# A selective scan's preparation, moved one slot ahead in a hand-written order of three interleaved streams

## The chip, the core and the metric

One core of a Trainium2 chip runs the whole program. Its engines work side by side, each on its own queue in order: TensorE (PE; its weight loads, PEld, overlap with it), VectorE (DVE), ScalarE (ACT), GpSimd (POOL) and SyncE (SP), which issues the DMAs. Semaphores tie them together. The metric is the time of the program on the device in microseconds (us).

## The reference

The input is 8 sequences of 512 tokens, 128 wide. Six layers run one after the other: a mixture of 8 experts (ffn 0), a Mamba layer, ffn 0 again, a second mixture of experts, windowed attention, and that mixture again. The change touches the Mamba layer, which for each sequence computes, cut to what matters:

```
h  = layernorm(layernorm(x)) * gamma + beta      # 512 tokens x 128
xi, z = split(h @ in_proj_w)                     # 256 wide each
xi = silu(causal_conv4(xi) + conv_b)             # four taps for each channel
dt, B, C = split(xi @ x_proj_w)                  # 8, 16, 16 wide
dt = softplus(dt @ dt_proj_w + dt_proj_b)
state = exp(dt * A) * state + (dt * xi) * B      # 16 states for each channel, token by token
y  = (sum over states of state * C) + xi * D
out = gelu((y * silu(z)) @ out_proj_w); gated linear unit; + skip
```

The first ffn 0 must be done with a sequence before Mamba prepares it, and the second ffn 0 follows Mamba on it.

## The kernel before

The first half of the program is the function `front`. It weaves three streams: A (ffn 0, first time), M (Mamba, function `mamba`) and F (ffn 0, second time). Time is cut into slots. On each engine's queue the instructions stand slot by slot, and within a slot in the order A, M, F. There is no barrier between slots; a slot is a place in the order, and each engine runs as far ahead as its semaphores let it.

**A and F.** One step is one 128-wide piece of one expert's hidden layer: three matmuls of 128x512 up (L123 to L125, PE), a relu (L390, ACT), and, two steps later, the product down, four 128x128 blocks in eight matmuls (L359, PE). After every fourth step DVE adds the expert's result, weighted, to the residual (L418). A sequence is 32 steps. F makes one step a slot, from slot 110 on. A's steps per slot are given by `pace`: 1 up to slot 56 but for two slots with 2, then 5 in 3 slots up to 110, then 4 in 5. A's last step comes near slot 244. Late in F and A one bank of PSUM each holds the up product and one the down product, so the next up product waits for the relu, and the next expert's down product for DVE's accumulation.

**M.** Sequence s takes the slots 56 + 32 s to 87 + 32 s; "slot 12 of sequence 3" is the 13th of these. The streams of M are written with v = slot - 56. In each slot, one of 16 states and one half (128 channels) of the inner width are worked on: ACT makes the decay exp(dt * A) one slot ahead (L798), POOL makes db = du * B three ahead (L808), DVE scans (L813) and multiplies by C (L828, `times_c`), and two slots later POOL adds the product to y (L839). SP loads B and C rows spread over the partitions (L529).

Beside this, M prepares the next sequence, s + 1, during sequence s, and ends the last one, s - 1. The class `Side` does it: a preparation is a generator per engine, and a tuple of slot numbers says in which slots its pieces are issued. `PREP_PE`, `PREP_ACT`, `PREP_DVE` and `PREP_POOL` are those of the preparation, the `TAIL_` tuples those of the end. The pieces of the preparation, in the order of the data:

- DVE: statistics and mean (L74, L80). It waits for A to be done with the sequence. POOL: six small operations to scales (L591 to L598).
- ACT: xm, the normalised tokens (L659, four activations). PE: T, four transposes (L114). DVE: hT (L716).
- PE: in0 (L626). DVE: c03 to c00, the four taps of half 0 (L723, L726), which read PSUM and u. ACT: t0, a tanh (L666). The same for half 1: in1, c13 to c10, t1. Between t0 and t1 ACT makes skip (L672).
- DVE: u0 and u1, the second step of silu (L730).
- PE: x, the product with x_proj_w (L634, two fp32 products in four matmul records). It waits for u1. ACT: two copies out of PSUM (L680 is one). DVE: lo, the small part of dt for a second product (L733). SP: B and C rows go to DRAM at slot 23.
- PE: dt0, dt1. ACT: the steps to softplus. DVE: sp0, sp1 (L737) in slot 28. POOL: du (L602). PE: in2, in3, the z part (L649), ACT and DVE after it.

All products of the preparation and the tail use one bank, XM. The tail of s - 1 has the output product (L748) in PE's slot 5, the two gated products gl0 and gl1 (L758, L759) in slots 6 and 8, ACT's gelu and two tanhs (sg0, sg1, L776) in slots 5, 6 and 8, DVE's go0 and go1 (L789) in slots 7 and 9. T must wait for go1, the last to read the bank. In M's part of a slot the tail's piece stands ahead of the preparation's.

F's own preparation for its next sequence falls, by its offsets, into M's slots 12 to 19: on DVE its statistics in 12, four small operations in 17 and four in 19; its accumulation is in every slot 3, 7, 11, 15, 19 and so on.

Of the kernel before, what the change touches and what calls it, by code (L numbers as in the profile page):

```python
# [222 lines left out]
def ffn0(S, C, sb, W, tag, x_at, x_ready, acc_at, acc_ready, hbank, ybank, HB, YB, XB, late=0):  # L223
# [23 lines left out]

    PREP_PE, PREP_ACT, PREP_POOL = (25, 27), (24, 25, 25, 28), (23,)
    PREP_DVE = (22, 22, 25, 27, 27, 27, 27, 29, 29, 29, 29)
    SLOTS = range(-12, END + 7)  # L250
# [82 lines left out]
    def pe(eng):  # L333
        side = Side(eng, prep_pe, PREP_PE)
        for v in SLOTS:
# [43 lines left out]
    def act(eng):  # L379
        side = Side(eng, prep_act, PREP_ACT)  # L380
        for v in SLOTS:
            s, j = divmod(v, NJ)
            if 0 <= v < END:
                e, c = divmod(j, HC)
                if v == 0:
                    eng.wait_ge(W["b1_at"].sem, W["b1_at"].at(0))
                if v >= NR:
                    eng.wait_ge(y_done.sem, y_done.at(v - NR))
                eng.wait_ge(up_done.sem, up_done.at(v))
                eng.activation(hf[v % NR][:], HB[hbank(v)].psum[:], ACT.Relu, bias=W["b1"][:, e, c:c + 1]).then_inc(relu.sem)  # L390
                if j == 2:
                    if s >= 1:
                        eng.wait_ge(bias_p.sem, bias_p.at(s - 1, "mm"))
                    eng.wait_ge(bias_p.sem, bias_p.at(s, "T"))
                    eng.copy(mkT[:], XB.psum[0:NT * E, 0:P]).then_inc(bias_a.sem)
            side.step(v)
            yield

    def dve(eng):
        side = Side(eng, prep_dve, PREP_DVE)  # L400
        for v in SLOTS:
            J = v - LEAD - late
            s, j = divmod(J, NJ)
            if 0 <= J < END:
                e, c = divmod(j, HC)
                q = s % 2
                if c == HC - 1:
                    eng.wait_ge(y_done.sem, y_done.at(J))
                    if e == 0:
                        eng.wait_ge(pd.sem, pd.at(s, "mk"))  # L410
                        eng.wait_ge(*acc_ready(s))
                    elif e == 1:
                        eng.wait_ge(bias_d.sem, bias_d.at(s))
                    else:
                        eng.wait_ge(acc_done.sem, acc_done.at(s * E + e - 1))
                    Y = YB[ybank(J // HC)].psum
                    for k in range(NT):
                        x = eng.scalar_tensor_tensor(acc_at(s)[:, k, :], Y[:, k * P:(k + 1) * P], mk[q][:, k, e:e + 1], acc_at(s)[:, k, :], ALU.mult, ALU.add)  # L418
                    x.then_inc(acc_done.sem)
                if j == HC:  # L420
                    eng.wait_ge(bias_p.sem, bias_p.at(s, "mm"))
                    eng.wait_ge(acc_done.sem, acc_done.at(s * E))
                    eng.tensor_tensor(acc_at(s)[:], acc_at(s)[:], XB.psum[:].rearrange("p (k d) -> p k d", d=D), ALU.add).then_inc(bias_d.sem)
            side.step(v)
            yield

    def pool(eng):
        side = Side(eng, prep_pool, PREP_POOL)
        for v in SLOTS:
            side.step(v)  # L430
            yield
# [11 lines left out]
def mamba(S, C, sb, a, cleared, x_at, x_ready, o_at, o_free, rows_dram, DH, XM):  # L443
# [51 lines left out]

    PREP_PE = (10, 12, 16, 21, 23, 25, 27, 30)
    PREP_ACT = (9, 15, 17, 19, 22, 22, 24, 24, 24, 25, 26, 26, 27, 27, 27, 30)
    PREP_DVE = (7, 7, 11, 13, 13, 14, 14, 17, 17, 18, 18, 19, 20, 22, 28, 28, 29, 31)  # L500
    PREP_POOL = (8, 28, 28)
    TAIL_PE, TAIL_ACT, TAIL_DVE, TAIL_POOL = (5, 6, 8), (5, 6, 8), (1, 1, 7, 9), (2, 2, 10)
    SLOTS = range(-NJ, END + 11)

# [46 lines left out]
    def pool(eng):  # L551
# [25 lines left out]
        eng.wait_ge(zeroed.sem, zeroed.at(0, "b_lo"))  # L577
        side, late = Side(eng, prep_pool, PREP_POOL), Side(eng, tail_pool, TAIL_POOL, 1)
        for v in SLOTS:
# [261 lines left out]
    def pe(eng):  # L841
        side, late = Side(eng, prep_pe, PREP_PE), Side(eng, tail_pe, TAIL_PE, 1)
        for v in SLOTS:
            if v == -NJ:
                eng.wait_ge(vec_ld.sem, vec_ld.at(4))
                eng.transpose(XM.psum[:, 0:8], rows[0:8, :], C["ident"][0:8, 0:8]).then_inc(rows_T.sem)
                XM.free = (ready.sem, ready.at(0, "cols"))
            late.step(v)
            side.step(v)
            yield  # L850

    def act(eng):
        side, late = Side(eng, prep_act, PREP_ACT), Side(eng, tail_act, TAIL_ACT, 1)
        for v in SLOTS:
            if v == -NJ:
                eng.wait_ge(mat_ld.sem, mat_ld.at(13))
                eng.activation(a_neg[:], a_neg[:], ACT.Exp).then_inc(a_exp.sem)
            if 0 <= v + 1 < END:
                decay(eng, v + 1)
            late.step(v)  # L860
            side.step(v)
            yield

    def dve(eng):
        side, late = Side(eng, prep_dve, PREP_DVE), Side(eng, tail_dve, TAIL_DVE, 1)
        for v in SLOTS:
            if v == -NJ:
                eng.wait_ge(rows_T.sem, rows_T.at(0))
                eng.tensor_copy(cols[:], XM.psum[:, 0:8]).then_inc(ready.sem)
                eng.wait_ge(ready.sem, ready.at(0, "cols"))  # L870
                eng.tensor_scalar(cols[:, DV:DV + NH], cols[:, DV:DV + NH], 0.5, None, ALU.mult).then_inc(ready.sem)
                eng.wait_ge(a_exp.sem, a_exp.at(0))
                eng.tensor_scalar(a_neg[:], a_neg[:], -1.0, None, ALU.mult).then_inc(ready.sem)
            if 0 <= v < END:
                scan(eng, v)
            if 0 <= v < END:
                times_c(eng, v)
            late.step(v)
            side.step(v)
            yield  # L880
# [13 lines left out]
def front(nc, S, C, bank, lasting, xin, a, f0, K, w1, sorted_rows):  # L894
# [3 lines left out]
    NJ, LM, LB = E * HC, 56, 110  # L898
# [3 lines left out]
    def pace(slot):  # L902
        if slot < LM:

            return 1 + (LM - 27 <= slot < LM - 25)
        return 1 + (slot % 3 != 0) if slot < LB else int(slot % 5 != 0)

    with ExitStack() as ctx, ExitStack() as scan_ctx:
# [16 lines left out]


        slots_of_first = [slot for slot in range(-12, 2 * END) for _ in range(pace(slot))]

        def slot_of_first(v):
# [9 lines left out]

        padding = S.count("f0_padding_cleared", 1, ("w_x", "w_dt", "b2"))  # L940
        M = mamba(S, C, sb_scan, a, padding, x_of, lambda s: A["done"](s), x_of, lambda s: M["x_read"](s), rows_dram, DH, XM)
        scan_end = nc.sbuf_base
        scan_ctx.close()
# [48 lines left out]
        def pool(eng):  # L992
            eng.memset(zero_row[:], 0.0).then_inc(zeroed.sem)
            weave((-12, A["pool"](eng), pace), (0, split_experts(eng)), (LM - NJ, M["pool"](eng)), (LB - 12, F["pool"](eng)))
            eng.wait_ge(*M["done"](NSEQ - 1))
            for i, e in enumerate([E] + list(range(E))):
                for u in range(NU):
                    k, hi, lo = NU * i + u, K["up_hi"][u][:, e, :], K["up_lo"][u][:, e, :]
                    eng.wait_ge(raw_ld[k % 4].sem, raw_ld[k % 4].at(k // 4))
                    eng.tensor_copy(hi, A["spent"][k % 4]).then_inc(split.sem)  # L1000
                    eng.wait_ge(split.sem, split.at(k, "hi"))
                    eng.tensor_tensor(lo, A["spent"][k % 4], hi.bitcast(F32), ALU.subtract).then_inc(split.sem)
# [20 lines left out]
        def act(eng):  # L1023
            weave((-12, A["act"](eng), pace), (LM - NJ, M["act"](eng)), (LB - 12, F["act"](eng)), (LN, norms_act(eng)))
# [1229 lines left out]
```

## Time and profile before

The median of three runs is 1887.43 us (1886.67 to 1887.5).

| what | value |
|---|---|
| time of the profiled execution | 1886.88 us |
| its span, first to last instruction | 1885.1 us |
| PE busy, share of the span | 1736.4 us, 92% |
| DVE busy | 1255.5 us, 67% |
| ACT busy | 1101.3 us, 58% |
| POOL busy | 1208.4 us, 64% |
| first and last scan (L813) start | 129.9 and 1019.8 us |
| POOL adds a product into y (L839), 240 times | mean 1.306 us |
| mean granted clock of PE | 0.976 of full speed |

The profile is one execution. A busy share is an average over stages with different limits. "Idle before" is the time an engine stood before an instruction, with what ended it; idle time of an engine that isn't the bound of its stage costs nothing. The granted clock is 1.0 at 2.4 GHz and 0.5 at 1.2 GHz; a stretch that has some of both lies between. The scans take 890 of the 1885 us; the front ends at 1117, and the second mixture and attention follow, which the change doesn't touch.

### The profile page before, as it was taken

The numbers are of one execution on the slowest core, as the hardware profiler recorded it, in microseconds if no ns is written. First come the engines' busy times: TensorE is split into PE (matmuls) and PEld (weight loads), VectorE is DVE, ScalarE is ACT, GpSimd is POOL, SyncE is SP. The second block draws the span as 40 slices with busy tenths as digits, with TensorE's granted clock in tenths as the row PEclk, the third lists the DMA queues.
The fourth block names the chain that finished last, engine by engine and source line by source line (L and its number), as shares of the span: only waits on it lengthen the run. The fifth ranks groups of instructions, "written<-read, shape, count | busy, mean of one in ns | idle before, by whom it ended". The sixth has DMA issues, their size and how long they took to land. (4 is left out here: it accounts for less than half of the span.)

```text
span 1885.1 us, 35637 instructions
## 1 busy us (share of the span) xinstructions
PE 1736.4 (92%) x12089; PEld 1507.4 (80%) x12089; DVE 1255.5 (67%) x2932; ACT 1101.3 (58%) x1937; POOL 1208.4 (64%) x1199
## 2 busy tenths in 40 slices
PE   7999898898989989988788999999899999999998
PEld 6888777787877777876567887888799999987887
DVE  2358889777797877879887437444477766656443
ACT  3476766666656766666665554343577777653442
POOL 3238787776777867779897716465556555544663
PEclk9999999999999999999889999999899999999999
DMA  5023333332223233332231501112454435201113
GB/s 148 1 75 116 101 105 94 98 97 90 97 83 112 94 104 93 93 99 85 84 95 42 151 7 50 36 48 62 137 179 140 123 114 155 68 21 39 47 50 103
DMA packets 121358, 166.71 MB, mean 88 GB/s; under 512 B 14646, under 2 KB 56604, under 8 KB 121180
## 3 DMA queue, kind: packets, MB, share of 16 engines
q1 hardware_dynamic: 114140, 148.82, 25.9%
q0 software_dynamic: 7040, 15.60, 2.6%
q8 instruction: 101, 1.65, 0.4%
q14 instruction: 77, 0.63, 0.1%
HBM read 114.17 MB, written 50.20 MB: 87 GB/s over the span
## 5 line engine op out<-in xcount | busy, mean ns | idle before, releaser
L808 POOL TENSOR_TENSOR db<-du_m,bt 128x512 f32<-128x512 f32 x256 | 328.4, 1284 | 140.9 <-DVE bank L813 140.4
L813 DVE TENSOR_TENSOR_SCAN bank<-bank,db 128x512 f32<-128x512 f32 x256 | 312.5, 1221 | 11.4 <-ACT bank L798 11.2
L839 POOL TENSOR_TENSOR y_m<-y_m,ph 128x512 f32<-128x512 f32 x240 | 313.4, 1306 | 0.3 <-DVE ph L828 0.3
L798 ACT ACTIVATE bank<-dt_m,a_neg 128x512 f32<-128x512 f32 x256 | 176.1, 688 | 84.9 <-DVE ph L828 78.9
L828 DVE TENSOR_TENSOR ph<-bank,ct 128x512 f32<-128x512 f32 x240 | 165.9, 691 | 8.6 <-POOL y_m L839 0.5
L1329 POOL TENSOR_TENSOR s_a<-s_a,mx_a 128x768 f32<-128x768 f32 x64 | 94.2, 1472 | 87.1 <-DVE mx_a L1412 87.1
L1443 PE MATMUL bank<-vb_a,pT_a 96*128 96x64 f32 x1024 | 121.6, 272 | 0.0
L1443 PEld LDWEIGHTS bank<-vb_a,pT_a 96*128 96x128 f32 x1024 | 119.6, 192 | 0.1
L359 PEld LDWEIGHTS bank<-dn,hf1b 128*128 128x128 f32 x680 | 91.2, 196 | 17.5 <-DVE x_all L418 7.8
L359 PEld LDWEIGHTS bank<-dn,hf2b 128*128 128x128 f32 x680 | 91.3, 196 | 16.4 <-DVE x_all L418 6.6
L359 PE MATMUL bank<-dn,hf1b 128*128 128x128 f32 x680 | 92.8, 281 | 7.9 <-DVE x_all L418 6.0
L359 PEld LDWEIGHTS bank<-dn,hf0b 128*128 128x128 f32 x688 | 90.6, 193 | 11.2 <-DVE x_all L418 2.7
L359 PE MATMUL bank<-dn,hf2b 128*128 128x128 f32 x680 | 92.7, 280 | 7.0 <-DVE x_all L418 4.9
L359 PEld LDWEIGHTS bank<-dn,hf1a 128*128 128x128 f32 x680 | 91.7, 196 | 8.1 <-DVE x_all L418 0.4
L359 PEld LDWEIGHTS bank<-dn,hf2a 128*128 128x128 f32 x680 | 90.7, 194 | 7.6
L359 PEld LDWEIGHTS bank<-dn,hf0a 128*128 128x128 f32 x688 | 90.0, 191 | 7.5 <-DVE x_all L418 0.2
L359 PE MATMUL bank<-dn,hf0b 128*128 128x128 f32 x688 | 92.0, 277 | 2.0 <-DVE x_all L418 1.5
L359 PE MATMUL bank<-dn,hf1a 128*128 128x128 f32 x680 | 92.1, 280 | 0.0
L359 PE MATMUL bank<-dn,hf2a 128*128 128x128 f32 x680 | 91.1, 278 | 0.0
L390 ACT ACTIVATE hf0a<-bank,b 128x512 f32<-128x512 f32 x86 | 58.9, 685 | 55.0 <-PE bank L125 54.5
L359 PE MATMUL bank<-dn,hf0a 128*128 128x128 f32 x688 | 90.6, 275 | 0.0
L390 ACT ACTIVATE hf1a<-bank,b 128x512 f32<-128x512 f32 x85 | 58.2, 685 | 53.2 <-PE bank L125 53.1
(469 smaller groups left out, 4872.9 us busy)
## 6 DMA issues: line engine op xcount, KB each, us to landing
bt<-bc_rows SPq DMA_DIRECT2D x128, 256.0 KB, 3.5
ct<-bc_rows SPq DMA_DIRECT2D x128, 256.0 KB, 3.4
sorted<-zero_row SPq DMA_DIRECT2D x64, 288.0 KB, 4.0
k_strips_a<-k_rows SPq DMA_DIRECT2D x32, 256.0 KB, 3.1
q_strips_a<-q_rows SPq DMA_DIRECT2D x32, 256.0 KB, 3.8
q_rows<-q_hi_a SPq DMA_DIRECT2D x16, 256.0 KB, 3.0
q_rows<-q_lo_a SPq DMA_DIRECT2D x16, 256.0 KB, 3.2
k_rows<-k_hi_a SPq DMA_DIRECT2D x16, 256.0 KB, 3.3
```

What stands on the lines that cost most here:

```text
L359: x = eng.matmul(Y.psum[:, t], hf[r][:, t], W["dn"][:, e, c, :], start=c == 0 and k == 0, stop=c == HC - 1 and k == NT - 1, skip_group_che ...
L390: eng.activation(hf[v % NR][:], HB[hbank(v)].psum[:], ACT.Relu, bias=W["b1"][:, e, c:c + 1]).then_inc(relu.sem)
L798: eng.activation(DH[J % 2][:], dt[s % 2][:, j % NH, :], ACT.Exp, scale=a_neg[:, j % NH, j // NH:j // NH + 1]).then_inc(da_done.sem)
L808: eng.tensor_tensor(db[J % RD][:], du[s % 2][:, j % NH, :], bt[N % RB][:], ALU.mult).then_inc(db_done.sem)
L813: eng.tensor_tensor_scan(DH[J % 2][:], DH[J % 2][:], db[J % RD][:], 0.0, ALU.mult, ALU.add).then_inc(hs_done.sem)
L828: eng.tensor_tensor(out, DH[J % 2][:], ct[N % RB][:], ALU.mult).then_inc(ph_done.sem)
L839: eng.tensor_tensor(y[s % 2][:, j % NH, :], y[s % 2][:, j % NH, :], ph[J % RP][:], ALU.add).then_inc(ys_done.sem)
L1329: eng.tensor_tensor(X[:], X[:], M[:, :, None].to_broadcast([P, UB, KW]), ALU.subtract).then_inc(sub_done.sem)
L1443: x = eng.matmul(BO[:, at:at + 2 * GD], pT[u % 2][:, c * BB + j, :], vb[s % 2][:, b:NB + 1:NB - b, g * GD:(g + 1) * GD], start=True, stop= ...
```

## The change

Every piece of the preparation from the statistics up to u1 is issued one slot earlier, on all four engines: T, in0, in1 on PE; xm, t0, skip, t1 on ACT; everything from the statistics to u1 on DVE; the scales on POOL. x on PE and what comes after it stay in their slots. So that A is still done with sequence 0 before M's first statistics, which now come one slot earlier (slot 30), A makes two steps in slot 28 too.

```diff
-    PREP_PE = (10, 12, 16, 21, 23, 25, 27, 30)
-    PREP_ACT = (9, 15, 17, 19, 22, 22, 24, 24, 24, 25, 26, 26, 27, 27, 27, 30)
-    PREP_DVE = (7, 7, 11, 13, 13, 14, 14, 17, 17, 18, 18, 19, 20, 22, 28, 28, 29, 31)
-    PREP_POOL = (8, 28, 28)
+    PREP_PE = (9, 11, 15, 21, 23, 25, 27, 30)
+    PREP_ACT = (8, 14, 16, 18, 22, 22, 24, 24, 24, 25, 26, 26, 27, 27, 27, 30)
+    PREP_DVE = (6, 6, 10, 12, 12, 13, 13, 16, 16, 17, 17, 18, 19, 22, 28, 28, 29, 31)
+    PREP_POOL = (7, 28, 28)
...
     def pace(slot):
         if slot < LM:
 
-            return 1 + (LM - 27 <= slot < LM - 25)
+            return 1 + (LM - 28 <= slot < LM - 25)
         return 1 + (slot % 3 != 0) if slot < LB else int(slot % 5 != 0)
```

LM is 56, the slot of the first scan, and LB is 110.

## Rows read from the trace of the kernel before

**Rows 1.** Waits of PE, slots 0 to 255: total, times, longest, us

```profile
PE bank L634 <- DVE u_m L730: 18.6, 5, 9.9
```

**Rows 2.** Windows: sequences 4, 6; then ffn b alone; busy PE, PEld, DVE, ACT, POOL

```profile
601.50:723.60 122.10, 112.94 (x693) 94.13 (x692) 97.92 (x197) 80.52 (x135) 90.46 (x81) 0.97 0.31 97
...
841.30:939.70 98.40, 76.84 (x406) 61.85 (x407) 87.68 (x149) 60.98 (x101) 87.51 (x77) 0.86 0.29 89
...
1021.70:1110.00 88.30, 87.87 (x582) 77.48 (x581) 34.46 (x157) 44.70 (x72) 40.23 (x44) 1.00 0.27 82
```

**Rows 3.** Windows, DVE alone, slot 13 to u1's end: sequence 4, sum of seven

```profile
649.00:679.72 30.72, 29.88 (x65) 0.97 0.32 98
...
sum 209.84, DVE 202.03; mean DVE 28.86
```

**Rows 4.** Windows, DVE alone, slot 12 of sequences 0 to 5

```profile
164.04:165.90 1.86, 1.82 (x3) 1.00 0.44 142
...
278.58:284.71 6.13, 4.68 (x18) 1.00 0.40 136
...
400.80:405.45 4.65, 3.66 (x13) 1.00 0.39 120
...
524.17:527.24 3.07, 2.99 (x13) 1.00 0.51 149
...
642.21:649.00 6.79, 4.80 (x17) 1.00 0.24 85
...
768.06:771.12 3.06, 2.98 (x13) 1.00 0.85 220
```

**Rows 5.** Instructions on u_m: least/median/most ns, first and last start, forms

```profile
L726 DVE SCALAR_TENSOR_TENSOR u_m<-bank,conv_w,u_m x48: 736/748/751, 88.6 to 897.9; 128x511 f32<-128x511 f32 x16, 128x510 f32<-128x510 f32 x16, 128x509 f32<-128x509 f32 x16
...
L723 DVE TENSOR_SCALAR u_m<-bank,conv_w,cols x16: 801/802/810, 87.8 to 891.7; 128x512 f32<-128x512 f32 x16
...
L730 DVE SCALAR_TENSOR_TENSOR u_m<-du_m,u_m x16: 682/1254/1273, 100.8 to 905.3; 128x512 f32<-128x512 f32 x16
```

**Rows 6.** The page, costliest groups: busy us, mean ns, idle before

```profile
L828 DVE TENSOR_TENSOR ph<-bank,ct 128x512 f32<-128x512 f32 x240 | 165.9, 691 | 8.6 <-POOL y_m L839 0.5
```

**Rows 7.** Timeline of PE: first x matmul of sequences 0, 1, 4, 6

```profile
196.75 2.08 PE L634 MATMUL bank<-u_m,w_x 128*128 128x512 f32 x2 [2.81 <-DVE u_m L730]
...
314.81 2.82 PE L634 MATMUL bank<-u_m,w_x 128*128 128x512 f32 x4 [2.39 <-DVE u_m L730]
...
679.77 2.08 PE L634 MATMUL bank<-u_m,w_x 128*128 128x512 f32 x2 [2.68 <-DVE u_m L730]
...
906.56 1.22 PE L634 MATMUL bank<-u_m,w_x 128*128 128x512 f32 x1 [9.89 <-DVE u_m L730]
```

**Rows 8.** Timeline of slot 19, sequence 2: start, us, engine

```profile
429.71 1.11 DVE L418 SCALAR_TENSOR_TENSOR x_all<-bank,mk0b,x_all 128x128 f32<-128x128 f32 x4
...
430.92 1.18 PE L359 MATMUL bank<-dn,hf1b 128*128 128x128 f32 x8 [1.94 <-issue]
```

**Rows 9.** Windows behind the x waits of sequences 1 and 4

```profile
315.70:319.00 3.30, 3.30 (x7) 1.91 (x6) 3.20 (x5) 1.85 (x3) 3.20 (x4) 0.52 0.01 2
...
677.50:684.20 6.70, 4.42 (x6) 2.18 (x7) 5.85 (x7) 0.69 (x1) 6.20 (x5) 0.51 0.08 32
```

**Rows 10.** Timeline of slots 7 to 10, sequence 4

```profile
625.51 0.86 DVE L74 BATCH_NORM_STATS2 stats_m<-x_all 128x6 f32<-128x128 f32 x4
...
635.05 0.41 DVE L789 SCALAR_TENSOR_TENSOR x_all<-sg,bank 128x256 f32<-128x256 f32 x1
...
637.16 0.60 PE L114 MATMUL bank<-ident,xm_m 128*128 128x128 f32 x4
```

**Rows 11.** Timeline of sequence 6, slots 6, 19 and 22

```profile
860.87 1.23 DVE L813 TENSOR_TENSOR_SCAN bank<-bank,db 128x512 f32<-128x512 f32 x1 [3.53 <-ACT bank L798]
...
901.05 1.72 POOL L839 TENSOR_TENSOR y_m<-y_m,ph 128x512 f32<-128x512 f32 x1
...
912.72 0.68 DVE L733 TENSOR_TENSOR xdb<-bank,xdb 32x512 fp32r<-32x512 f32 x1 [2.48 <-ACT xdb L680]
```

## The prediction

> **What bounds the kernel now.** I read the windows by sequence of the scan first. In sequence 4 PE is busy 112.94 of 122.10 us and DVE 97.92; in sequence 6, where ffn a has ended, PE has 76.84 of 98.40 and DVE 87.68 [rows 2]. So PE bounds sequences 1 to 5 over the whole, DVE bounds sequences 6 and 7, and when the scan is over ffn b fills PE alone: 87.87 of 88.30 us, with 582 matmuls at 11 a step, so 1.67 us a step [rows 2]. An idle PE in sequences 0 to 5 is lost time; in sequence 6 only a DVE stall is.
>
> The mean hides an alternation, which the second view, DVE's busy time in chosen stretches, shows. From the scan of slot 13 to the end of u1 in slot 20, DVE is busy 202.03 of 209.84 us over seven sequences (29.88 of 30.72 in sequence 4) [rows 3]. There DVE is the bound and PE waits for it. In slot 12, just ahead, DVE's idle time is 0.04, 1.45, 0.99, 0.08, 1.99 and 0.08 us in sequences 0 to 5 [rows 4].
>
> The third view is who PE waits for. The x product (L634) waits for DVE's u1 (L730) five times, 18.6 us, more than for anything else [rows 1]: 2.81 in sequence 0, 2.39 in 1, 2.68 in 4 and 9.89 in 6 [rows 7], and by subtraction 0.8 in 3. In sequence 2 x waits for nothing, because PE was held just before: its down product in slot 20 (L359) begins at 430.92 after 1.94 idle, right behind DVE's accumulation for ffn b in slot 19, 429.71 to 430.82 [rows 8]. These are the two ways out of the DVE stretch: through that accumulation, and through u1.
>
> **The change part by part.**
>
> *The same work, moved.* Nothing is added or removed. On DVE the statistics go to slot 6, hT to 10, the convolution's eight steps (0.80 for the first of each half, 0.75 for the others [rows 5]) to slots 12, 12, 13, 13, 16, 16, 17, 17, and u0, u1 (1.25 each [rows 5]) to 18 and 19. No DMA is issued by a moved step. SP's wait for bc stays at slot 23 behind an unmoved x. The distances between producer and consumer stay as they are up to u1; u1 to x grows from one slot to two.
>
> *Way out through the accumulation of slot 19.* Before it DVE had done u0 and now does u0 and u1: +1.25. Against that one conv pair, 0.80 + 0.75 = 1.55, leaves the stretch through its front, slot 12, and is free as far as DVE idled there. So the change per sequence is 1.25 less the idle of slot 12, at most 1.55: +1.21, -0.20, +0.26, +1.17, -0.30, +1.17. Where F is not yet active (0, 1) the same lateness reaches PE through the relu behind ACT's tanh. Nothing at all if PE is not held here is one end; +1.55 if slot 12 gives no room is the other.
>
> *Way out through u1.* x goes when u1 is done, now without slot 20's scan and product ahead of it, 1.23 + 0.69 = 1.92 [rows 6, 11], and from sequence 2 on without F's accumulation either, 1.11 [rows 8]. That covers the waits of 2.81 and 2.39 but for what the line before hands on: sequence 0: 1.21 - 2.81 = -1.6; 1: -0.2 - 2.39 = -2.6; 2: +0.3; 3: 1.17 - 0.8 = +0.4; 4: -0.3 - 2.68 = -3.0; 5: +1.2. The sum is -5.3 us. Its ends are -10 (no lateness at slot 19) and +4 (1.55 in each of six, x waits cut by half).
>
> *Sequence 6.* PE's 9.89 us are worth nothing by themselves, DVE bounds. But DVE itself idles 2.48 ahead of its split of xdb (L733), because x, the copy and thus the split are late, and 3.53 ahead of a scan in slot 6, for ACT's decay behind its table loads [rows 11]. x comes 3 us sooner: -2.4. The statistics (0.86, with their aggregation about 1.3: they begin at 625.51 [rows 10]) fall into the second gap: -1.3. Together -3.7; at least 0, if other waits of DVE take their place.
>
> *T next to the tail.* In PE's queue the four transposes of xm now stand in slot 9 right behind gl1 (slot 8) and need DVE's go1, which is in slot 9 too; behind them wait both ffns. In sequence 4 they began at 637.16 and go1 ended at 635.46 [rows 10]. One slot sooner is two ffn steps sooner, 637.16 - 2 x 1.67 = 633.8, so PE would stand 1.6 us. In sequences 1, 3 and 5 I find go1 and the new place within some tenths of each other; DVE gets there sooner by the statistics, which left slot 7 for idle time. I take +1.6 in all; the ends are 0 and 1.6 in each of six sequences, 9.6. On ACT xm's four steps follow sg1 at once and t0 comes ahead of F's normalisation; both are short of a stall by the same margin as before if DVE keeps its pace.
>
> *The pace.* A runs three double slots, not two: one step of 1.7 us is done before the scan begins, and one fewer before A ends, in slots that PE bounds. Net 0. It also shifts all of A's own waits by one step against the scan. What that does I can't price from a row; I allow 3 us to either side.
>
> *The clock.* Behind the x waits of sequences 1 and 4 the granted clock is 0.52 and 0.51, the lower level of 1.2 GHz, for 3.3 and 6.7 us [rows 9]; seven such stretches lie in slots 19 to 22 of sequences 0 to 5. Half of their PE time is what they cost, here 5.0 us in all. PE idles before some of them at slot 19 as well, so I take a third back: -1.7.
>
> *A port between DVE and POOL.* Beside u0 and u1 POOL's sum takes 1.72 us [rows 11], where the mean of its group is 1.31 (the table above). The Trainium skill (SBUF — State Buffer, "Who interferes with whom") says that a DVE operation with two SBUF inputs and a GpSimd operation lock each other out of a shared pair of ports for the whole instruction. The trace agrees as to the direction. By this rule the move changes nothing, since u0 and u1 meet a sum in any slot, while a conv step, with PSUM and one SBUF input, locks nobody out. It would speak against the change only if the small two-input operations of F in slots 17 and 19 were caught more often, and it gives no count.
>
> **The sum.** -5.3 - 3.7 + 1.6 - 1.7 = -9.1. What PE gains in slot 21 has to pass the slots 24 to 28, where ACT is nearly full, so I keep four fifths: -7.3. The profiled execution took 1886.88 us (span 1885.1, 1.8 around it), 0.55 under the median of 1887.43. From the median: 1880.1 us.
>
> **The rivals.**
>
> *Given back (about 1885.5).* PE leaves slot 21 sooner and then waits for a relu or an accumulation, because DVE and ACT are where they were: DVE's cumulated work at the start of slot 21 is the same to the microsecond. For it: 202.03 of 209.84 [rows 3]. Against it: after slot 21 DVE and ACT wait for PE again. Then only half of sequence 6 is left, -1.9.
>
> *The tail holds the transposes: slower (about 1892).* PE reaches T before go1 in all of sequences 1 to 6, 6 x 1.6 = +9.6. hT, the in-products and the first conv pair are late by as much, so slot 12's room isn't used: 6 x 1.25 = +7.5. Less x waits of 8.7 and sequence 6's 3.7: +4.7. It decides from the point where go1 ends more than about 1 us behind PE's arrival in most sequences; sequence 4 is past it [rows 10], three others stand on it.
>
> *The clock comes back whole (about 1870).* PE stands less in slots 19 to 21, none of the seven stretches at 1.2 GHz is left: 12 us of PE time where I took 1.7. For it: every one lies behind a wait of that place. Against it: the waits of slot 19 stay. The Trainium skill (TensorE: Matmul & The Clock Gate, "What's actually happening") has the clock gated down after PE was idle and up again after it was busy; by that rule whoever takes the gaps away gets the clock too. The trace agrees that gap and low clock go together.
>
> *It doesn't do what it says.* If other waits had ordered the engines, moving the steps by a slot would move nothing. DVE's queue is in order and full in the stretch, so I give this no chance of its own.
>
> **How the numbers follow.** Forecast 0.50 (its own range 1874 to 1885), given back 0.25, slower 0.17, clock 0.08. The range 1871 to 1893 takes in both small cases but for their outer ends. A measurement tells 0.2%, 3.8 us, from no change, so faster is below 1883.7: 0.47 of the forecast's, the clock's 0.08 and a little of the second, 0.58. Slower is above 1891.2: most of the third and a little of the chaos of A's shift, 0.17. Same: 0.25.
>
> **What would show it.** The wait of L634 for u_m falls from 18.6 us to under 7, nearly all of it in sequence 6. PE's idle at slot 19 (L359 behind L418) stays or grows by up to 1.2. Windows at clock 0.5 after slot 20 in sequences 1 and 4 are fewer. L733's 2.48 in sequence 6 is gone. L114 of xm waits for L789, about 2 us in all. It is wrong if that wait is over 8 us, if the stretch from the first scan to the last is no shorter, or if the part behind the front changes its length.

## The result, and the profile after

The change makes the kernel slower. The median after is 1898.17 us (1886.92 to 1907.2, 19 runs) against 1887.5 us for the kernel before in the same session (1880.7 to 1900.38, 19 runs): the ratio is 1.0055 with a 95% interval of 1.0042 to 1.0067, which on 1887.5 us is +10.4 us. 1880.1 was forecast; 1898.17 lies outside the range of 1871 to 1893 too. The profiled execution took 1898.17 us (span 1896.4), 11.3 more than that of before.

The page after, its line of busy times and that of POOL's sum into y:

```profile
PE 1749.2 (92%) x12089; PEld 1516.4 (80%) x12089; DVE 1254.9 (66%) x2932; ACT 1100.9 (58%) x1937; POOL 1207.3 (64%) x1199
...
L839 POOL TENSOR_TENSOR y_m<-y_m,ph 128x512 f32<-128x512 f32 x240 | 312.8, 1304 | 0.4 <-DVE ph L828 0.4
```

DVE, ACT and POOL work as long as before, to about a microsecond. PE is busy 12.8 us longer (1749.2 against 1736.4), with as many instructions. So the same matmuls ran slower. The mean granted clock of PE is 0.970 of full speed after and 0.976 before, so the clock, and not only the order, has a part in the loss.

The windows after, from first scan to first scan of the sequences 0 to 7, then ffn b alone, then the part behind the front (from, to, length; busy PE, PEld, DVE, ACT, POOL; granted clock, DMA share, GB/s). They answer to [rows 2]:

```profile
130.50:233.20 102.70, 98.09 (x635) 84.81 (x634) 92.76 (x175) 72.82 (x122) 83.36 (x73) 1.00 0.37 111
233.20:360.40 127.20, 110.84 (x640) 91.49 (x638) 100.71 (x207) 81.13 (x138) 93.95 (x87) 0.93 0.30 90
...
481.50:609.80 128.30, 115.52 (x690) 96.98 (x690) 98.10 (x189) 79.54 (x133) 92.74 (x82) 0.95 0.29 92
609.80:731.30 121.50, 113.11 (x704) 95.49 (x703) 100.18 (x200) 81.75 (x137) 89.35 (x80) 0.99 0.30 95
...
850.10:949.80 99.70, 79.31 (x406) 63.04 (x407) 87.19 (x149) 60.92 (x101) 87.84 (x77) 0.86 0.29 87
...
1029.90:1126.60 96.70, 96.09 (x641) 84.98 (x639) 37.48 (x164) 47.55 (x77) 41.76 (x46) 1.00 0.26 74
1126.60:1896.40 769.80, 732.36 (x5943) 657.66 (x5943) 431.91 (x1228) 411.09 (x798) 422.53 (x467) 0.99 0.28 84
```

Before, the same stretches lasted 104.1, 123.1, 120.5, 123.8, 122.1, 117.7, 98.4 and 80.1 us, ffn b alone 96.7 and the rest 768.6. Nearly the whole loss lies in the scan: 899.3 us from the first scan to the last, 889.9 before, so 9.4 of the 11.3; the part behind the front has 1.2 and the part ahead of the scan 0.6. Sequence 1 gives +4.1 and sequence 3 +4.5; sequences 5 and 6 give 1.1 and 1.3, and 0 and 4 are shorter by 1.5 and 0.6.

Within the scan PE stands idle 92.0 us; before it was 94.3. The idle time did not grow at all. But it is busy 11.8 us longer (the sum of the windows), and the record of the granted clock has it at 1.2 GHz for 88.8 us of the scan, before for 68.1. At half the clock products take up to twice as long (eight of L359 take 1.91 us for 1.06, below), so at most half of those 21 us, 10.4, is lost. The clock's column gives the same from rounded numbers: length times (1 - clock), summed over the eight windows, is 43.6 us after and 32.9 before.

The waits of PE in the scan after (total, times, longest). The third last answers to [rows 1]:

```profile
PE bank L359 <- DVE x_all L418: 14.1, 11, 3.7
PE bank L123 <- ACT hf0b L390: 12.2, 10, 3.2
...
PE bank L114 <- DVE x_all L789: 7.8, 3, 4.7
PE bank L643 <- DVE xdb L733: 7.0, 5, 3.9
...
PE bank L626 <- DVE u_m L726: 5.2, 3, 4.3
...
PE bank L634 <- DVE u_m L730: 3.8, 2, 2.5
...
PE bank L626 <- DVE hT L716: 1.1, 2, 0.6
```

x (L634) waits 3.8 us, before 18.6 [rows 1]. In place of the 14.8 that went, three waits have come or grown: T for go1 (L114, 7.8), dt0 for lo (L643, 7.0 against 0.9) and in1 for the last tap of half 0 (L626 for L726, 5.2 against none). Together they grew by 19.1. The wait of in0 for hT, the last row, fell from 3.1 to 1.1.

### The profile page after: what moved, and what is told of

Same layout as the page of the kernel before. It is cut to its first block and busy times, and to the rows that moved or that the text cites. A ratio compares the mean times of both kernels' runs of the same rounds, so it can differ in the third digit from the quotient of the medians.

```text
span 1896.4 us, 35637 instructions
## 1 busy us (share of the span) xinstructions
PE 1749.2 (92%) x12089; PEld 1516.4 (80%) x12089; DVE 1254.9 (66%) x2932; ACT 1100.9 (58%) x1937; POOL 1207.3 (64%) x1199
## 5 line engine op out<-in xcount | busy, mean ns | idle before, releaser
L839 POOL TENSOR_TENSOR y_m<-y_m,ph 128x512 f32<-128x512 f32 x240 | 312.8, 1304 | 0.4 <-DVE ph L828 0.4
L359 PEld LDWEIGHTS bank<-dn,hf1b 128*128 128x128 f32 x680 | 95.9, 205 | 17.8 <-DVE x_all L418 6.5
L359 PE MATMUL bank<-dn,hf1b 128*128 128x128 f32 x680 | 97.0, 289 | 7.7 <-DVE x_all L418 4.7
L359 PEld LDWEIGHTS bank<-dn,hf2b 128*128 128x128 f32 x680 | 89.5, 193 | 16.4 <-DVE x_all L418 7.5
L359 PEld LDWEIGHTS bank<-dn,hf0b 128*128 128x128 f32 x688 | 92.6, 197 | 10.6 <-DVE x_all L418 2.4
L359 PEld LDWEIGHTS bank<-dn,hf0a 128*128 128x128 f32 x688 | 91.9, 195 | 9.0 <-DVE x_all L418 1.4
L359 PEld LDWEIGHTS bank<-dn,hf2a 128*128 128x128 f32 x680 | 92.5, 198 | 7.9
L359 PE MATMUL bank<-dn,hf2b 128*128 128x128 f32 x680 | 90.8, 277 | 7.4 <-DVE x_all L418 6.2
L359 PEld LDWEIGHTS bank<-dn,hf1a 128*128 128x128 f32 x680 | 89.7, 192 | 8.8 <-DVE x_all L418 1.4
L359 PE MATMUL bank<-dn,hf0b 128*128 128x128 f32 x688 | 93.7, 281 | 1.5 <-DVE x_all L418 1.3
L359 PE MATMUL bank<-dn,hf0a 128*128 128x128 f32 x688 | 92.5, 278 | 0.9 <-DVE x_all L418 0.9
L390 ACT ACTIVATE hf1a<-bank,b 128x512 f32<-128x512 f32 x85 | 58.3, 685 | 59.5 <-PE bank L125 59.1
L359 PE MATMUL bank<-dn,hf2a 128*128 128x128 f32 x680 | 92.5, 281 | 0.0
L359 PE MATMUL bank<-dn,hf1a 128*128 128x128 f32 x680 | 90.3, 276 | 0.9 <-DVE x_all L418 0.9
L390 ACT ACTIVATE hf0a<-bank,b 128x512 f32<-128x512 f32 x86 | 58.9, 685 | 54.3 <-PE bank L125 53.5
```

Of the source, the lines that this page charges most:

```text
L359: x = eng.matmul(Y.psum[:, t], hf[r][:, t], W["dn"][:, e, c, :], start=c == 0 and k == 0, stop=c == HC - 1 and k == NT - 1, skip_group_che ...
L839: eng.tensor_tensor(y[s % 2][:, j % NH, :], y[s % 2][:, j % NH, :], ph[J % RP][:], ALU.add).then_inc(ys_done.sem)
```

## Where the time went: slot 9 of sequence 3

The largest of the new waits, in the timeline after (start, duration, engine; idle before and its releaser in brackets):

```profile
513.54 1.13 DVE L418 SCALAR_TENSOR_TENSOR x_all<-bank,mk1a,x_all 128x128 f32<-128x128 f32 x4 [2.07 <-PE bank L359]
...
514.58 0.61 DVE L321 TENSOR_TENSOR exa<-exa,sela 128x32 f32<-128x32 f32 x1
...
515.77 1.22 DVE L813 TENSOR_TENSOR_SCAN bank<-bank,db 128x512 f32<-128x512 f32 x1
517.02 0.69 DVE L828 TENSOR_TENSOR ph<-bank,ct 128x512 f32<-128x512 f32 x1
...
517.63 0.41 DVE L789 SCALAR_TENSOR_TENSOR x_all<-sg,bank 128x256 f32<-128x256 f32 x1
...
518.19 1.09 PE L114 MATMUL bank<-ident,xm_m 128*128 128x128 f32 x4 [4.69 <-DVE x_all L789]
...
520.36 1.91 PE L359 MATMUL bank<-dn,hf1b 128*128 128x128 f32 x8
520.65 0.69 ACT L390 ACTIVATE hf0b<-bank,b 128x512 f32<-128x512 f32 x1 [6.65 <-PE bank L125]
...
524.94 1.23 DVE L813 TENSOR_TENSOR_SCAN bank<-bank,db 128x512 f32<-128x512 f32 x1 [4.32 <-ACT bank L798]
```

And the same place before:

```profile
512.90 0.41 DVE L789 SCALAR_TENSOR_TENSOR x_all<-sg,bank 128x256 f32<-128x256 f32 x1
...
515.26 0.60 PE L114 MATMUL bank<-ident,xm_m 128*128 128x128 f32 x4
...
515.47 1.12 DVE L418 SCALAR_TENSOR_TENSOR x_all<-bank,mk1a,x_all 128x128 f32<-128x128 f32 x4 [2.15 <-PE bank L359]
...
518.00 0.78 DVE L330 SCALAR_TENSOR_TENSOR mk0a<-exa,dena 128x32 f32<-128x32 f32 x1
518.70 1.22 DVE L813 TENSOR_TENSOR_SCAN bank<-bank,db 128x512 f32<-128x512 f32 x1
```

Before, go1 came first, then T, and A's accumulation for ffn a (L418 with mk1a), which begins when PE has done the expert's last product, only in slot 10. After, that accumulation and A's routing behind it (L321 to L330) stand in slot 9, ahead of the scan and of go1: the third double slot of the pace has shifted all of A by a step. DVE waits 2.07 us for PE's product, then works through accumulation, routing, scan and product by C, and only then does go1, while PE has T next in its queue and stands 4.69 us. Each engine in turn waits for the other, with both full of other work that stands behind. ACT has the relu and the decay behind this, so DVE's scan waits 4.32 a little later: the wait shows on three engines.

It doesn't end with the wait. Windows of PE alone, ahead of the wait, in it and behind it (length, busy, clock):

```profile
505.00:513.50 8.50, 8.50 (x53) 1.00 0.27 91
513.50:518.20 4.70, 0.01 (x2) 0.86 0.05 16
518.90:524.20 5.30, 5.30 (x23) 0.55 0.55 152
```

Ahead of it PE was busy all the time at full clock; behind it it is busy all the time at 1.2 GHz, and eight products of L359 take 1.91 us instead of 1.06. In this sequence PE has 13.7 us at 1.2 GHz and had 3.4 before. Of its +4.5 us, PE's idle time makes 1.3 (12.8 against 11.5) and its busy time 3.2 (115.5 against 112.3): the 4.69 in part took the place of other waits, and the slower products are the larger part.

Sequence 1, with +4.1, is another matter, for T waits for nothing there. PE comes to dt0 2.5 us sooner than before (317.9 against 320.5), but ACT's copy (L680) is 2.1 us later and so is lo, and the clock behind this wait is low too. Lo before, lo after, and PE alone behind the wait:

```profile
318.51 0.68 DVE L733 TENSOR_TENSOR xdb<-bank,xdb 32x512 fp32r<-32x512 f32 x1
```

```profile
321.08 0.68 DVE L733 TENSOR_TENSOR xdb<-bank,xdb 32x512 fp32r<-32x512 f32 x1
```

```profile
322.00:326.00 4.00, 4.00 (x16) 0.57 0.58 143
```

This sequence has 17.1 us at 1.2 GHz after and 10.2 before.

## The experiments

Each kernel is timed against the kernel before in the same session, on the same chip. The three sessions had chips of different speed (1935.99, 1937.47 and 1885.27 us for the kernel before), so only ratios and the scan's own numbers are compared across them. The second profile of the kernel before is a single run. In the table "scan" is first to last scan, "idle" is PE's idle time in it, "1.2 GHz" the time at the lower clock in it, and the last columns are PE's waits for go1, u1, lo and half 0's last tap (L726), all us of one profiled execution. The expectations count the idle time gap by gap, which gives 2 to 4 us more (98 for before); the table has the length less the busy time. One execution is not the median: those of e2, e3 and e10 lie 10.1, 11.2 and 5.7 us below the median of their kernel, so a difference of a few us in the scan's columns that the ratio doesn't bear out shows nothing.

| kernel | ratio, 95% interval | scan | idle | 1.2 GHz | T | x | dt0 | in1 |
|---|---|---|---|---|---|---|---|---|
| before | 1 | 889.9 | 94.3 | 68.1 | 0 | 18.6 | 0.9 | 0 |
| e6_before_again | (one run) | 890.5 | 94.7 | 71.6 | 0 | 19.1 | 0.9 | 0 |
| after | 1.0055 [1.0042, 1.0067] | 899.3 | 92.0 | 88.8 | 7.8 | 3.8 | 7.0 | 5.2 |
| e5_change_again | 1.0037 [1.002, 1.0054] | 896.0 | 92.6 | 78.6 | 7.8 | 3.8 | 7.0 | 5.2 |
| e1_pace_alone | 1.0008 [0.998, 1.0036] | 889.2 | 95.7 | 71.6 | 1.2 | 26.5 | 0.7 | 0.6 |
| e2_move_alone | 1.0016 [0.9989, 1.0043] | 893.1 | 92.9 | 68.2 | 5.1 | 2.6 | 6.0 | 4.7 |
| e3_to_transposes | 1.0033 [1.0008, 1.0057] | 894.4 | 95.0 | 78.4 | 5.1 | 18.5 | 0.9 | 1.3 |
| e4_from_in1 | 1.0028 [1.0001, 1.0054] | 897.5 | 95.9 | 78.4 | 0 | 2.8 | 6.6 | 14.6 |
| e7_T_in_10 | 0.9962 [0.9942, 0.9983] | 886.4 | 84.9 | 78.4 | 1.8 | 4.1 | 6.2 | 5.2 |
| e8_tail_earlier | 0.9989 [0.9974, 1.0004] | 886.7 | 82.9 | 75.1 | 1.9 | 3.7 | 7.0 | 5.2 |
| e9_dt_in_24 | 0.9957 [0.994, 0.9975] | 880.4 | 84.1 | 68.2 | 1.8 | 4.1 | 0 | 5.2 |
| e10_old_pace | 0.9968 [0.9952, 0.9983] | 879.5 | 91.4 | 44.3 | 0.3 | 2.4 | 7.7 | 4.7 |
| e11_u_back | 1.0023 [1.0008, 1.0037] | 893.5 | 97.8 | 64.8 | 1.8 | 25.2 | 0.8 | 5.2 |
| e12_from_hT | 0.9977 [0.9959, 0.9995] | 886.0 | 90.2 | 64.7 | 0 | 3.9 | 6.0 | 4.7 |

### First session: the parts, one by one, on the kernel before

**e1_pace_alone.** Only the third double slot.

```diff
-            return 1 + (LM - 27 <= slot < LM - 25)
+            return 1 + (LM - 28 <= slot < LM - 25)
```

> Only the third double slot of A is kept; the preparation stays in its old slots. Theory P (the shift of A by one step against the scan is what costs): about 8 to 11 us slower than before, the whole loss. Theory T (the transposes of xm meet go1 in slot 9, PE stands and its clock falls): within 2 us of before. Theory C (the convolution, moved into slots 12 and 16, meets F's preparation): within 2 us of before.

Measured 1.0008, no difference; its interval ends at 0.36%, 7 us, short of the 8 to 11 that theory P expected. In sequence 3 A's accumulation stands ahead of go1 here too, but T is still in slot 10 and waits only 1.2 us. The pace by itself is not the cause.

**e2_move_alone.** The whole move for sequences 1 to 7 at the old pace; sequence 0 keeps the old slots, since A isn't done with it a slot sooner. `Side` takes a second tuple, `first`, for s = 0.

```diff
+            for _ in range((self.first if self.first and s == 0 else self.places).count(j)):
...
+    FIRST_PE = (10, 12, 16, 21, 23, 25, 27, 30)
+    PREP_PE = (9, 11, 15, 21, 23, 25, 27, 30)
```

> The whole preparation is one slot ahead for sequences 1 to 7; sequence 0 keeps the old slots, and so A keeps its old two double slots. Theory P: within 2 us of before, or faster by the 18.6 us x wait's share, -3 to -7. Theories T and C: 8 to 11 us slower than before, as the whole change.

Measured 1.0016, 3 us; the interval, -2 to +8 us, includes 1 and decides between no two of the theories. T waits 5.1 us (1.75, 1.47 and 1.90 in sequences 1, 4 and 6) and in sequence 3 not at all. With e1 that sets the interaction apart: the 4.69 came only with both the move of T and the shifted pace.

**e3_to_transposes.** The old pace and, for sequence 0, the old slots, as in e2; only statistics, scales, xm and T a slot ahead, from hT on as before.

```diff
+    PREP_PE = (9, 12, 16, 21, 23, 25, 27, 30)
+    PREP_ACT = (8, 15, 17, 19, 22, 22, 24, 24, 24, 25, 26, 26, 27, 27, 27, 30)
+    PREP_DVE = (6, 6, 11, 13, 13, 14, 14, 17, 17, 18, 18, 19, 20, 22, 28, 28, 29, 31)
+    PREP_POOL = (7, 28, 28)
```

> Old pace. Only statistics, scales, xm and the transposes T are one slot ahead (sequences 1 to 7); hT and all behind it stay. Theory T: 5 to 9 us slower than before, T waits for go1 some 6 to 8 us in all. Theory C: within 2 us of before. Theory P: within 2 us of before.

Measured 1.0033, slower by 6.4 us (1.5 to 11), which is what theory T expected. The two waits in its trace (here L789 is L794, and L634 and L730 are L639 and L735):

```profile
PE bank L639 <- DVE u_m L735: 18.5, 5, 9.6
...
PE bank L114 <- DVE x_all L794: 5.1, 3, 1.9
```

The x wait is what it was, and T's 5.1 us and 10 us more at 1.2 GHz have come. So moving T up to the tail costs time at the old pace too, if the statistics, scales and xm that moved with it cost nothing, which is not measured apart.

**e4_from_in1.** The old pace and sequence 0 as in e2; in1, the taps of half 1, skip, t1, u0 and u1 a slot ahead, what precedes them not.

```diff
+    PREP_PE = (10, 12, 15, 21, 23, 25, 27, 30)
+    PREP_ACT = (9, 15, 16, 18, 22, 22, 24, 24, 24, 25, 26, 26, 27, 27, 27, 30)
+    PREP_DVE = (7, 7, 11, 13, 13, 14, 14, 16, 16, 17, 17, 18, 19, 22, 28, 28, 29, 31)
```

> Old pace. Statistics to the first half's four taps and its tanh stay in their old slots; in1, the four taps of the second half (slots 16 and 17), skip, t1, u0 and u1 are one slot ahead (sequences 1 to 7). The x wait should fall from 18.6 to under 6 us. Theory T: faster than before by 3 to 7 us, since T stays where it was. Theory C: slower by 3 to 8 us. Theory P: faster by 3 to 7 us.

Measured 1.0028, but it doesn't say what it was to say. in1 overwrites what half 0's last tap reads, and was brought next to it: that wait is 14.6 us. It belongs to this experiment's way of dividing the change. Its +5 us is what theory C (the convolution meets F's preparation) expected, but e7, e10 and e12 have the same taps in slots 12, 13, 16 and 17 and are faster than before, so theory C is out. What is left is that a product next to the last reader of its bank waited in all seven sequences.

### Second session: undoing one part of the change

**e5_change_again and e6_before_again** are the kernels after and before, unchanged.

> The change as it is, once more, beside the kernel before on the chip of this call. If the parts are to be compared with the whole, it must be about 10 us (0.5%) slower here too. Theory K (PE waits as long as before, but its waits lie at other places and more stretches at 1.2 GHz follow them): PE's idle in the scan within 3 us of before's 98 us, low clock 80 to 95 us against 68. Theory T (T's wait for go1): T waits 6 to 9 us.

> The kernel before, a second profile: from first to last scan 889.9 us within 3 if the front is repeatable to that; its stretches at 1.2 GHz in the scan 60 to 76 us in all (68.1 in the first profile).

The change again gives 1.0037, and its interval overlaps with the first; it is 7 us and not 10. The four waits of the table are the same to 0.1 us (that of the output product for POOL's y is not: 1.2 and 3.3), and sequences 0 to 5 last the same to 0.1. Sequence 6 lasted 96.8 us instead of 99.7, with 10 us less at 1.2 GHz. The kernel before repeats as expected: 890.5 and 71.6 for 889.9 and 68.1. So these waits are the kernel's, and a part of the low clock differs from one execution to the next.

**e7_T_in_10.** The change, but T stays where it was.

```diff
-    PREP_PE = (9, 11, 15, 21, 23, 25, 27, 30)
+    PREP_PE = (10, 11, 15, 21, 23, 25, 27, 30)
```

> The change, but PE's transposes T stay in slot 10 (hT is in slot 10 of DVE already). Theory T: T's wait of 7.8 us for go1 is gone, and 5 to 9 us of the loss with it: 1 to 5 us slower than before. Theory P (shift of A): still 8 to 11 us slower. Theory K: T's wait is gone, in0 (L626) waits more for hT; total idle the same, 4 to 9 us slower than before.

Measured 0.9962: one number of the change decides its sign. Against the change in the same session it is 1932.01 to 1945.34 us, -13.3, and more than 7 even between the near ends of the two intervals. Theory T expected a gain of 5 to 9 and a kernel still slower than before; it came out faster. The waits:

```profile
PE bank L643 <- DVE xdb L733: 6.2, 5, 3.9
PE bank L626 <- DVE u_m L726: 5.2, 3, 4.3
...
PE bank L634 <- DVE u_m L730: 4.1, 2, 2.9
...
PE bank L114 <- DVE x_all L789: 1.8, 2, 1.5
```

T waits 1.8 instead of 7.8 us, the other three stay within 0.8, and PE's idle time falls by 7.7. The scan is 9.6 shorter. The time at 1.2 GHz is the same in these two profiles, 78.4 and 78.6, so here the difference lies in the waits and not in the clock. Sequence 3 is shorter by 4.9 us (123.3), 4 and 5 by 2.0 and 2.5; sequence 1 is not (128.3).

**e8_tail_earlier.** The change, and the tail from the output product on one slot ahead too, so that go1 keeps its distance from T.

```diff
-    TAIL_PE, TAIL_ACT, TAIL_DVE, TAIL_POOL = (5, 6, 8), (5, 6, 8), (1, 1, 7, 9), (2, 2, 10)
+    TAIL_PE, TAIL_ACT, TAIL_DVE, TAIL_POOL = (4, 5, 7), (4, 5, 7), (1, 1, 6, 8), (2, 2, 9)
```

> The change with the tail one slot earlier too on PE, ACT and for DVE's go0, go1 and POOL's fin, so that T stands as far behind go1 as before. Theory T: T's wait under 2 us, 0 to 5 us slower than before. Theory K: waits move once more (the output product in slot 4 waits for POOL's y), total idle 95 to 102 us, time anywhere within 8 us of the change. Theory P: no better than the change.

Measured 0.9989, the interval just includes 1. T's wait falls to 1.9 and PE's idle time by 9.7, as in e7. But now the output product (L748) waits 5.6 us for POOL's y (L609), against 1.2 and 3.3 in the two profiles of the change: PE sits before the tail instead of behind it. Two ways of parting T from go1 both take the loss away (9.3 us here, 13.3 in e7).

### Third session: from e7 on

**e9_dt_in_24.** e7, with dt0 a slot later, away from lo.

```diff
-    PREP_PE = (10, 11, 15, 21, 23, 25, 27, 30)
+    PREP_PE = (10, 11, 15, 21, 24, 25, 27, 30)
```

> The change with T in slot 10, and PE's first dt product in 24 instead of 23, where ACT's step behind it already stands. The dt product waited 6.2 us for DVE's lo. If such a wait is lost time: 2 to 5 us faster than with T in 10 alone, whose ratio to before was 0.9962, so 0.993 to 0.996. If PE's waits only move (theory K): the same as T in 10 alone, 0.995 to 0.998, with the wait gone and PE's total idle as it was, 87 us.

Measured 0.9957 [0.994, 0.9975], 1877.04 us: the fastest of all, and faster than before and after. That dt0's move helps is not shown, for the interval is e7's as well. Its wait is gone from the list, but PE's idle time is 84.1 after 84.9. The waits for the relus (L123 for L390, both ffns) went from 31.9 to 36.9 us: the idle time moved on. In sequence 1 the 3.87 us of dt0 became 3.85 us in front of an up product at the same place.

**e10_old_pace.** e7 for sequences 1 to 7 at the old pace, sequence 0 in its old slots (the `first` of e2).

> The change with T in slot 10, A's two double slots as before, and sequence 0 prepared in the old slots. Tells what the shift of A costs where T is out of the way. Theory P: 3 to 6 us faster than with the new pace (0.993 to 0.995). Without it: 0.995 to 0.998, sequences 1 and 3 as with T in 10 (128 and 123 us) within 2 us.

Measured 0.9968, as e7. So with T away from go1 the pace makes no difference that can be told, and theory P, with 0.993 to 0.995, is out. Its profile has a scan of 879.5 us and only 44.3 at 1.2 GHz with 91.4 idle, so the profiled execution looks better (-10.4) than the ratio (-6); it was the fastest of 12. In it sequences 1 and 3 took 120.8 and 120.4 us, not 128 and 123 within 2 as expected. How much of that is the pace stays open.

**e11_u_back.** e7 with u0 and u1 back in slots 19 and 20, next to x.

```diff
-    PREP_DVE = (6, 6, 10, 12, 12, 13, 13, 16, 16, 17, 17, 18, 19, 22, 28, 28, 29, 31)
+    PREP_DVE = (6, 6, 10, 12, 12, 13, 13, 16, 16, 17, 17, 19, 20, 22, 28, 28, 29, 31)
```

> The change with T in slot 10, but u0 and u1 on DVE back in slots 19 and 20. The prediction's step on x: the x wait comes back, 4 to 15 to 19 us, and the front is 4 to 8 us longer than with T in 10 alone (886.4 between the scans): ratio 0.998 to 1.001. If x's wait was never on the path: ratio 0.995 to 0.998, PE's idle back at 95 us or more without a longer scan.

Measured 1.0023, just above the range expected. The x wait is back, in full:

```profile
PE bank L634 <- DVE u_m L730: 25.2, 7, 7.6
...
PE bank L643 <- DVE xdb L733: 0.8, 3, 0.5
```

Between e11 and e7, which ran on different chips, lie 0.61%, 11.5 us, for these two operations; between e11 and e10, on one chip but with the old pace, 10.4. 21.1 us of waiting went and 5.4 came at dt0. The gain of the change is real and sits here. The rest of the move, without T and without u0 and u1, is 0.23% slower than before.

**e12_from_hT.** The kernel before with only hT, in0, in1, the taps, the tanhs, u0 and u1 ahead; statistics, scales, xm, T and the pace as before.

```diff
+    PREP_PE = (10, 11, 15, 21, 23, 25, 27, 30)
+    PREP_ACT = (9, 14, 16, 18, 22, 22, 24, 24, 24, 25, 26, 26, 27, 27, 27, 30)
+    PREP_DVE = (7, 7, 10, 12, 12, 13, 13, 16, 16, 17, 17, 18, 19, 22, 28, 28, 29, 31)
```

> The kernel before with only hT to u1 one slot ahead: statistics, scales, xm and T in their old slots, the old pace. Theory T: like T in 10, 0.995 to 0.998 (the statistics' move is worth nothing). If the statistics' move into DVE's gap in slot 6 is what T in 10 gains by: 0.999 or more. Theory P: faster than T in 10 alone.

Measured 0.9977. Its interval overlaps with those of e7, e9 and e10. What the earlier statistics add (0.1% between e12 and e10, which also differ in sequence 0) can't be told from nothing.

## Why the prediction was wrong

**The step that failed is "T next to the tail", +1.6 us.** It saw the right place, go1 beside T, and the right price in sequence 4 (1.22 measured for 1.6). It put sequences 1, 3 and 5 at "within some tenths", and sequence 3 had 4.69. That reading was wrong by the prediction's own rule: before, T of sequence 3 began at 515.26, two steps sooner is 511.9, and go1 ended at 513.31, so it stood 1.4 us short, like sequence 4 (sequences 1 and 5 come to 0.6 and 0.3). Two things more were left out of the term. The first is that the change moves A against M by a step, and so moves what stands ahead of go1 on DVE. "The pace: net 0, can't price" was booked as a term of its own, when its effect is on this one: alone it costs nothing that shows (e1), T's wait without it is 5.1 (e2), with it 7.8 (e5). It could have been priced from the trace of before, where A's accumulation began 2.2 us behind go1's end (512.90 + 0.41 to 515.47) and needed only one step to be ahead. The second is that a wait of PE was priced at its own length and no more. With T back in slot 10 the time falls by 13.3 us for 6.0 of wait (e7 to e5), and T ahead on the kernel before, with the statistics and xm, costs 0.33%, 6 us, for 5.1 (e3). Of the three signs of being wrong, T's wait stayed just under its 8 us, at 7.8; the scan, 9.4 us longer, gave the sign.

**The clock, -1.7, had the wrong sign.** The rival that expected it back whole needed the gaps to go. They didn't: 94.3 us idle became 92.0, in other places, and the time at 1.2 GHz rose by 21 us. The rule of the Trainium skill (TensorE: Matmul & The Clock Gate, "What's actually happening") that this rival names, gated down after PE was idle and up again after it was busy, agrees with sequence 3: 4.7 us with PE idle, then a clock of 0.55. The new gap in sequence 3 is a long one behind a full stretch, and the trace shows the lower clock right behind it. Which of the other gaps brought the lower clock is shown by their place alone, and it is only partly the kernel's (e5's sequence 6). The term's base was also too large: the two stretches of [rows 9] hold 3.30 and 4.42 us of PE time, and half of that is 3.9, not 5.0.

**x, and the way out through the accumulation, -5.3, were right in kind.** Their size isn't measured by itself; e11 and e7 give 11.5 us for u0 and u1 where everything else has moved. The x wait fell to 3.8 us (under 7 as said, but not nearly all of it in sequence 6: 2.53 there, 1.26 in sequence 1). Timeline of PE after, sequences 1 and 6, which answer to [rows 7]; the second row is dt0:

```profile
313.67 1.98 PE L634 MATMUL bank<-u_m,w_x 128*128 128x512 f32 x4 [1.26 <-DVE u_m L730]
321.82 0.50 PE L643 MATMUL bank<-xdb,w_dt 96*128 96x512 f32 x1 [3.88 <-DVE xdb L733]
...
915.57 3.16 PE L634 MATMUL bank<-u_m,w_x 128*128 128x512 f32 x4 [2.53 <-DVE u_m L730]
```

The room of slot 12 was used. DVE alone from slot 12, where the stretch now starts, to the end of u1 in slot 19, sequence 4 and the sum of seven, which answer to [rows 3]:

```profile
655.64:687.26 31.62, 30.51 (x66) 0.95 0.21 70
...
sum 207.16, DVE 199.20; mean DVE 28.46
```

It is as full as before, 96%, and a slot earlier. PE's waits for the accumulation (L418) grew from 12.4 to 14.1 in all; in sequence 2, slot 19 [rows 8], from 1.94 to 3.01, within the "up to 1.2".

**"Given back" took more than was granted.** The rival said that PE would leave slot 21 sooner and stand further on. That is dt0 in sequence 1: x goes 1.1 us sooner, PE reaches dt0 2.5 us sooner, and lo on DVE comes 2.6 us later. Of the 14.8 us of x, 6.1 came back at dt0 and 5.2 at in1. in1's wait was in no term: the prediction said that the distances up to u1 stay, in slots, which they do, but in sequence 6 half 0's last tap is now 4.28 us behind PE.

**Sequence 6, -3.7, didn't show**: it is 1.3 longer in the first profile and 1.6 shorter in the second, depending on the clock. L733's 2.48 of idle time [rows 11] is gone as said. T's 1.89, in1's 4.28 and x's 2.53 stand in its place.

**The port, no effect, fits**: POOL's sum takes 1304 ns, before 1306.

**The sum.** Without the T step the forecast was -10.7 before the four fifths. The kernel without T's move (e7) gives -0.38%, on 1887 us -7.2. With the four fifths they come to -8.6, so they were about right in all. One by one they weren't (the clock has the wrong sign in e7 too, 78.4 us against 71.6 at 1.2 GHz), so that is partly luck. The slower rival, "the tail holds the transposes", named the mechanism; it had +4.7 for +10.4. Its condition, T reached before go1 in all six sequences, was met in three. Its other half, hT's lateness, doesn't show: in0 waits 2 us less for hT.

**Open.** How much of the 10.4 us is the clock. By the first pair of profiles it is all, by the second (e6 to e5: scan +5.5, 7 us more at 1.2 GHz) about two thirds, between e5 and e7 nothing. In the second pair PE is busy 7.6 us longer, of which the clock's record explains 3.5. The waits repeat and the clock's stretches do so in part; more profiles of one kernel would tell. Nor was T's move tried with A's accumulation kept behind go1 at the new pace, so the part of that accumulation is read from the timeline and from e1 and e2, while the part of T's slot is shown by e7 and e8. What keeps sequence 1 long at the new pace is open too.

## What to carry to other kernels

When a step moves by a slot, write down for each engine what stands in the queue ahead of the instruction it waits for, after the move, with every other stream shifted as the change shifts it: two edits, neither of which costs anything clear of noise alone (e1, e2), can meet in one slot. Leave a product that overwrites a shared bank a slot away from the bank's last reader, even if everything else moves; here that one number turned +0.4% into -0.4%. And don't price a gap at its length alone. A new one in a full PE stretch can have slower products behind it (sequences 1 and 3). A removed one gives what doesn't turn up at the next dependency: 13.3 us for T's 6.0, 11.5 for x's 21.1, and nothing that could be told for dt0's 6.2.

## What the runs showed of the hardware

In before, after and e1 to e6 the idle time of PE in the scan hardly moves with the order of the work (92.0 to 95.9 us), while the scan lasts from 889.2 to 899.3. What differs there is how long the same matmuls take, and the time at 1.2 GHz (68.1 to 88.8 us) is the one cause of it that was found. With T away from go1 the idle time does fall, to 82.9 to 84.9 in e7, e8 and e9.

Four waits of PE of 2.4 to 4.7 us had the lower clock right behind them: 2.39 us and then 0.52, 2.68 and then 0.51 ([rows 7] and [rows 9], before), 3.88 and then 0.57, 4.69 and then 0.55 (after). The 1.26 us for x in sequence 1 after did not: from 313.67 to 316.00 the granted clock is 1.00.

The front repeats nearly exactly, from one chip to another too: six sequences within 0.1 us in two profiles of the change, seven of eight in two of the kernel before (sequence 1 has 123.1 and 123.7). Yet the chips of the first two sessions took about 50 us longer for the same kernel (1936 and 1937 against 1885 and 1887), and all of it lies behind the front: 807 to 824 us there instead of 766 to 770. A part that is identical in all kernels can differ more than any change here makes, so only ratios from one chip count.
